# Gate logits as eight more columns of the output product, routing one step earlier

## The reference, cut to what matters

```python
x = x + tanh(g_xattn[0]) * xattn(layernorm(x), ctx, ctx, W_qkv, b_qkv, W_out, b_out)   # 16 heads of 8
x = x + tanh(g_ffn[0])   * moe(layernorm(x), Wg, W1, b1, W2, b2)

# moe: 8 experts, each takes at most 512 of the 4096 tokens, in token order
logits = tokens @ Wg
gates  = softmax(logits);  idx = argmax(gates)
mask1  = one_hot(idx);     loc = cumsum(mask1, axis=0) - 1        # place within the expert
mask1  = mask1 * (loc < 512)
out    = gates1 * (relu(token @ W1[e] + b1[e]) @ W2[e] + b2[e])   # for tokens that got a place
```

## Time and profile before

| | us |
|---|---|
| median of three runs | 356.81 |
| the three runs | 352.88, 356.81, 358.24 |
| the profiled execution | 352.81 |
| its span in the profile | 351.0 |

### The profile page before, as it was taken

One profiled execution on the slowest core, in us unless ns is written; L12 is line 12 of the kernel. 1 busy time (PEld: TensorE's weight loads), 2 busy tenths in 40 slices (PEclk: granted clock), 3 DMA queues, 4 the chain that ended last, 5 costly groups with the idle time before them and its releaser, 6 DMA issues.

```text
span 351.0 us, 8166 instructions
## 1 busy us (share of the span) xinstructions
PE 261.1 (74%) x2960; PEld 169.0 (48%) x2960; DVE 201.8 (57%) x696; ACT 158.5 (45%) x357; POOL 173.4 (49%) x202
## 2 busy tenths in 40 slices
PE   0348698888996995996896888969331899999920
PEld 0124445545654654654654555635220366777720
DVE  6244649778895895568687597932320144544520
ACT  7253376865764763564674456551010332322100
POOL 5336724757179179238728625070462005555572
PEclk9999999999998998589899699995555699999985
DMA  2984765615244235208217111074014225664300
GB/s 79 294 222 110 229 183 149 182 32 162 64 115 129 66 91 152 63 3 230 51 29 209 43 56 64 5 200 76 30 51 130 71 64 162 186 200 142 89 37 21
DMA packets 48536, 39.26 MB, mean 112 GB/s; under 512 B 9619, under 2 KB 44072, under 8 KB 48497
## 3 DMA queue, kind: packets, MB, share of 16 engines
q1 hardware_dynamic: 44784, 28.67, 30.5%
q0 software_dynamic: 3712, 10.07, 8.6%
HBM read 13.72 MB, written 12.65 MB: 75 GB/s over the span
## 4 chain that ended last, share of the span: by engine, by line
POOL 26%; issue 26%; PE 22%; ACT 8%; DVE 7%; DMA 5%; SPq 2%; POOLq 1%; ACTq 0%; DVEq 0%
POOL rec_dram L1002 7%; POOL out_dram L1056 6%; POOL rs L982 4%; PE O L489 3%; PE X L418 3%; ACT prob L623 2%; ACT xn L615 2%; DVE negm L734 2%; POOL rec L988 2%; PE S L460 2%; POOL rec L990 2%; PE X L412 2%; PE TS L561 2%; PE X L435 2%; DMA qp<-parts_q 2%
## 5 line engine op out<-in xcount | busy, mean ns | idle before, releaser
L734 DVE TENSOR_REDUCE negm<-S 128x4 f32<-128x512 f32 x128 | 81.8, 680 | 27.5 <-PE S L460 26.5
L623 ACT ACTIVATE prob<-TS 128x512 f32<-128x512 f32 x128 | 72.0, 589 | 47.5 <-PE TS L475 47.3
L489 PE MATMUL O<-prob,vals 128*32 128x128 f32 x1024 | 58.1, 303 | 1.6 <-ACT oraw L632 1.6
L460 PE MATMUL S<-kp,qp 62*128 62x128 bf16 x512 | 33.5, 234 | 5.2 <-DVE negm L734 4.7
L1056 POOL DMA_INDIRECT out_dram<-fin,tok x32 | 31.3, 979 | 11.2 <-issue 11.2
L1002 POOL DMA_INDIRECT rec_dram<-rec,slot x32 | 31.8, 994 | 9.7 <-issue 9.7
L256 POOL TENSOR_TENSOR rest_k<-full_k,parts_k 128x512 f32<-128x512 f32 x7 | 8.1, 1155 | 53.4 <-ACT parts_k L606 53.4
L489 PEld LDWEIGHTS O<-prob,vals 128*32 128x32 f32 x1024 | 21.3, 113 | 21.7 <-issue 10.9
L975 POOL TENSOR_TENSOR fence_p<-pool_c 128x1 f32<-128x1 f32 x16 | 3.1, 194 | 56.7 <-DVE fin L955 34.3
L460 PEld LDWEIGHTS S<-kp,qp 62*128 62x128 bf16 x512 | 19.2, 100 | 23.5 <-issue 11.7
L475 PE MATMUL TS<-qp,kp 64*128 64x128 bf16 x512 | 28.9, 228 | 1.3 <-DMA qp<-mrow 1.3
(11 more groups left out here) (115 smaller groups left out, 513.1 us busy)
## 6 DMA issues: line engine op xcount, KB each, us to landing
kp<-parts_k SPq DMA_DIRECT2D x48, 128.0 KB
qp<-parts_q SPq DMA_DIRECT2D x48, 128.0 KB, 2.7
rec_dram<-zeros POOLq DMA_DIRECT2D x8, 516.0 KB
xr<-rec_dram SPq DMA_DIRECT2D x8, 260.0 KB, 2.9
c_sb<-in_ctx_dram SPq DMA_DIRECT2D x8, 256.0 KB, 4.4
out_dram<-rec SPq DMA_DIRECT2D x8, 256.0 KB
w1s<-in_L_ffn_W_dram SPq DMA_DIRECT2D x8, 256.0 KB, 3.1
w2s<-in_L_ffn_W_dram SPq DMA_DIRECT2D x8, 256.0 KB, 2.9
```

The lines of the kernel that those rows point to most:

```text
L460: mm = nc.tensor.matmul(S[:, a, i * L:(i + 1) * L], qp[b][rows, h, t0:t0 + L], kp[b][rows, h, t0:t0 + L], start=True, stop=True)
L489: mm = nc.tensor.matmul(o_out[i * HV:(i + 1) * HV, u * L:(u + 1) * L], vals[G % 2][:, k, h, :], prob[n % 2][:, h * L:(h + 1) * L], start=( ...
L623: nc.scalar.activation(prob[n % 2][:, first:first + 4 * L], TS[:, a, :], ACT.Exp).then_inc(a_exp, 1)
L734: V.tensor_reduce(negm[n % 2][:, first:first + 4], S[:, a, :].rearrange("p (h k) -> p h k", k=L), AX.X, ALU.max, negate=True).then_inc(v_r ...
```

## The change

**Logits by linearity.** The output product `onT x wout_g` gets 8 more columns, so that it is [128 x 136]. The added columns of the weights are W_out (times its gain) times the centred gate weights, wg_c = Wg less its mean over the features; they are worked out once, in steps 0 and 1, by two transposes and two small products, and wg_c by a product with a constant matrix in step -6. x's part of the logits comes from the transposed normalised x that the q product uses anyway: a task xl (four matmuls into 8 columns each, step j=0) and one DVE operation (x_logits), which multiplies by the standard deviation sd1. The result stands beside x in x_sb, which has 136 columns now, and so the addition of line 765 yields x1 and the raw logits at once.

**Taken out** in each group: PE's transpose of the second norm (nT, 4 transposes), ACT's copy of it (669), the logits product (lg, 4 matmuls) and DVE's copy (842).

**Added** in each group: xl on PE, x_logits, a second operation in offset1 (sd1) and `scaled` (logit differences times 1/std) on DVE.

**Moved.** route from j=2 to j=0, directly after the group's last residual; pos from j=3 to j=1 (and from 14 small matmuls to 5); place from j=3 to j=2; the exponential from j=2 to j=1; x's statistics and their aggregation from j=0 and j=1 of one group to j=3 of the group before; root(g+2) ahead of norm2(g-2) on POOL; ACT's first half of x's normalisation ahead of the last two exponentials of step j=1. The scatter of group 6 no longer stands behind norm2 of group 7. The bias is added to x one group later.

**The start.** The context of group 0 is loaded second. x is loaded group by group. The statistics of group 0 wait for x alone; the weights are reordered without the gains; the first q split is DVE's instead of POOL's; two of the three q buffers are cleared by POOL instead of ACT; two DVE fills come later; records of zeros are written in steps 1 to 8.

```diff
@@ x_tasks
-            third = {2: ("lg", g - 2), 3: ("pos", g - 2)}.get(j)
+            third = {0: ("xl", g), 1: ("pos", g - 2)}.get(j)
-            second = {1: ("nT", g - 2), 2: ("xT", g + 2), 3: ("q", g + 2)}.get(j)
+            second = {2: ("xT", g + 2), 3: ("q", g + 2)}.get(j)
@@ PE tasks
-                elif name == "nT":
-                    pe.wait_ge(g_xn2, idx + 1)
+                elif name == "xl":
                     for k in range(GB):
-                        mm = nc.tensor.transpose(X[:, 0, k * L:(k + 1) * L], rec[idx % 3][:, k, 0:D], ident)
-                elif name == "lg":
-                    pe.wait_ge(a_nT, idx + 1)
-                        mm = nc.tensor.matmul(X[:, 1, k * E:(k + 1) * E], xn2T[:, k * L:(k + 1) * L], wg_sb[:],
+                        mm = nc.tensor.matmul(X[:, 1, k * E:(k + 1) * E], xnT[idx % 2][:, k * L:(k + 1) * L], wg_c[:],
@@ PE step
-                    nc.tensor.matmul(X[:, 0, 0:D], onT[(c - 5) % 2][:], wout_g[:], start=True, stop=True).then_inc(p_at, 1)
+                    nc.tensor.matmul(X[:, 0, 0:DE], onT[(c - 5) % 2][:], wout_g[:], start=True, stop=True).then_inc(p_at, 1)
@@ DVE
+                V.tensor_tensor(sd1[H % 2][:], rs1[:, 0, :], rs1[:, 1, :], ALU.mult).then_inc(v_sd, 1)
+            def x_logits(H):
+                V.tensor_tensor(x_sb[:, H * GB:(H + 1) * GB, D:DE], X[:, 1, 0:GB * E].rearrange("p (k e) -> p k e", e=E),
+                                sd1[H % 2][:].unsqueeze(2).broadcast_to([P, GB, E]), ALU.mult).then_inc(v_xl, 1)
+            def scaled(G):
+                dve.wait_ge(v_lraw, G + 1)
+                dve.wait_ge(g_rs2, G + 1)
+                V.tensor_tensor(ldif[:], ldif[:], rs2[:, 1, :].unsqueeze(2).broadcast_to([P, GB, E]), ALU.mult).then_inc(v_ldif, 1)
@@ DVE step (order of the group parts)
+                if j == 2 and is_group(g - 2):
+                    positions(g - 2)
                 if is_batch(c):
                     top(c, 0)
 ...
+                if j == 0 and is_group(g):
+                    x_logits(g)
+                if j == 0 and is_group(g - 2):
+                    route(g - 2)
+                if j == 1 and is_group(g - 2):
+                    scaled(g - 2)
                 if j == 2 and is_group(g - 2):
-                    logits(g - 2)
-                if j == 3 and is_group(g - 2):
-                    positions(g - 2)
-                if j == 2 and is_group(g - 2):
-                    route(g - 2)
-                if j == 3 and is_group(g - 2):
                     place(g - 2)
-                if j == 0 and is_group(g + 2):
-                    moments1(g + 2)
+                if j == 3 and is_group(g + 3) and g + 3 >= 2:
+                    moments1(g + 3)
+                    gathered1(g + 3)
@@ POOL step
+                if j == 0 and is_group(g + 2) and g + 2 >= 2:
+                    root(g + 2, mv1, rs1, v_mv1, g_e1).then_inc(g_rs1, 1)
                 if j == 0 and is_group(g - 2):
                     norm2(g - 2)
-                if j == 0 and g - 3 == NG - 2:
-                    scatter(NG - 2)
 ...
-                if j == 3 and is_group(g - 2) and g - 2 != NG - 2:
+                if j == 3 and is_group(g - 2):
                     scatter(g - 2)
@@ SP
-            sp.dma_start(x_sb[:, 0:GB, :], x_v[:, 0:GB, :]).then_inc(x_in[0], 16)
+            sp.dma_start(x_sb[:, 0:GB, 0:D], x_v[:, 0:GB, :]).then_inc(x_in[0], 16)
+            sp.dma_start(c_sb[0][:], ctx_v[:, 0:GB, :]).then_inc(c_in[0], 16)
 ...
-                if c == -7:
-                    sp.dma_start(x_sb[:, 2 * GB:, :], x_v[:, 2 * GB:, :]).then_inc(x_in[2], 16)
+                if j == 1 and 2 <= g + 3 < NG:
+                    rows = slice((g + 3) * GB, (g + 4) * GB)
+                    sp.dma_start(x_sb[:, rows, 0:D], x_v[:, rows, :]).then_inc(x_in[g + 3], 16)
```

More of the change, by code:

```diff
@@ L110, in flamingo_kernel @@
         xn = sb("xn", [P, GB, D])
-        xnT = sb("xnT", [P, GT])
+        xnT = [sb(f"xnT{i}", [P, GT]) for i in range(2)]
         st1 = sb("st1", [P, GB, 6])
@@ L115, in flamingo_kernel @@
         nm1 = sb("nm1", [P, GB])
+        sd1 = [sb(f"sd1_{i}", [P, GB]) for i in range(2)]
         full = [sb(f"full_{s}", [P, GT]) for s in "qk"]
@@ L132, in flamingo_kernel @@
         rs2 = sb("rs2", [P, 2, GB])
[L133 to L135 removed]
+        rec = [sb(f"rec{i}", [P, GB, D + DE]) for i in range(3)]
         lmax = sb("lmax", [P, GB])
@@ L346, in step @@
                     sp.dma_start(out_v[:, sl, :], rec[(g - 2) % 3][:, :, D:2 * D]).then_inc(x1_out[(g - 2) % 3], 16)
-                if loads:
+                if loads and g + 2 >= 1:
                     if g + 2 >= 2:
@@ L498, in step @@
                 at_q = {0: [t for t in groups if t[0] in ("v", "cT") or t[0] == "k" and j == 3], 1: [],
-                        2: [t for t in groups if t[0] in ("lg", "pos", "xT", "q") or t[0] == "k" and j == 2],
-                        3: [t for t in groups if t[0] == "nT"]}
+                        2: [t for t in groups if t[0] in ("xT", "q", "xl") or t[0] == "k" and j == 2],
+                        3: [t for t in groups if t[0] == "pos"]}
                 if is_batch(c):
@@ L652, in step @@
                         first_part(1, 0)
-                if j == 2 and is_group(g + 2):
+                if j == 2 and is_group(g + 2) and g + 2 != 0:
                     normed1(g + 2, (2, 3)).then_inc(a_xn, 1)
+                if c == -5:
+                    act.wait_ge(s_vset, 2)
+                if c == -4:
+                    act.wait_ge(s_gain, 32)
+                    nc.scalar.activation(tg[:], gains[:], ACT.Tanh).then_inc(s_tanh, 1)
+                if j == 1 and is_group(g + 2) and g + 2 >= 2:
+                    normed1(g + 2, (0, 1))
                 if is_batch(c - 2):
@@ L685, in step @@
                     nc.scalar.activation(lexp[:], ldif[:], ACT.Exp).then_inc(a_lexp, 1)
-            for i in range(3):
-                nc.scalar.memzero(qp[i][:]).then_inc(a_pad, 1)
-            act.wait_ge(s_bias, 96)
-            nc.scalar.activation(tg[:], gains[:], ACT.Tanh).then_inc(s_tanh, 1)
-            act.wait_ge(s_vset, 1)
+            nc.scalar.memzero(qp[0][:]).then_inc(a_pad, 1)
             run_steps(step)
@@ L895, in step @@
                     split(dve, V, 1, 0)
-                if j == 0 and is_group(g + 2):
-                    moments1(g + 2)
-                if j == 1 and is_group(g + 2):
-                    offset1(g + 2)
-            for i in range(3):
-                V.memset(kp[i][:].rearrange("p h n -> p (h n)").bitcast(F32), ONES_B).then_inc(v_pad, 1)
-            dve.wait_ge(s_cst, 16)
-            V.tensor_copy(ident_b[:], ident)
-            V.tensor_copy(before_b[:], cst[:, P:2 * P])
-            V.memset(ones_b[:], 1.0)
@@ new lines, in step @@
+                if c == -5:
+                    gathered1(1)
+                    split(dve, V, 0, 0)
+                    offset1(1)
+                if c == -8:
+                    moments1(0)
+                if j == 3 and is_group(g + 3) and g + 3 >= 2:
+                    moments1(g + 3)
+                    gathered1(g + 3)
+                if c == -7:
+                    offset1(0)
+                if c == -7:
+                    dve.wait_ge(s_bias, 64)
+                    V.tensor_scalar(bq_s[:], bqk[:, 0:1], SCALE, None, ALU.mult).then_inc(s_vset, 1)
+                    ones_in(1)
```

220 lines of the change are left out of this document (133 added, 87 removed).

## The result

| | us |
|---|---|
| kernel before, median of five runs | 355.73 |
| changed kernel, median of five runs | 346.10 (345.17 to 348.01) |
| ratio | 0.9753, 95% interval 0.9713 to 0.9792 |
| span of the changed kernel's profiled execution | 346.2 (before 351.0) |

A forecast was written before the change was run, and what follows sets the result against it. PE's waits for POOL's norm2, the lower clock after them and the last group's chain were taken to bound the kernel; terms summing to -32.6 us took 352.81 to 320.2, plus 1 gave 321 us, range 309 to 335.

The forecast's parts named there:

- the 1 us put on the distance of profile and median: Added to the forecast execution of 320.2 us, giving 321; the earlier median lay 4.0 us above the profiled execution.
- to c = 1: Start: earlier loads and statistics, shorter q split on DVE, first score at about 24.6; -6 us (-8 to -3).
- c = 1 to 13, weights folded: Loop before the stalls: added DVE work and xl, +2 us (0 to +4); weight folding, +1 (0 to +2).
- c = 13 to 25: Three stalled groups: 24.5 us each, DVE busy 23.3 setting the pace, against 84.18 in all; -10.7 (-14.3 to -4.7).
- c = 25 to 29: Stretch from 187.29 to 211.96: one stall and lower clock go, 21.0 us instead of 24.67; -3.7 (-5 to -2).
- c = 29 to 32: Stretch from 211.96 to 227.96: shorter stall and routing leave, 14.2 us instead of 16.0; -1.8 (-2.5 to -0.5).
- end of the stage: From 227.96 to 270.88: last scatter starts at 247.5 rather than 260.88; -13.4 us (-16 to -7).
- experts: Expert stage, 80.12 us: not touched by the change.
- rival D: Loop and end: a 3.4 us PE wait per group remains, through the context transpose; 348 to 354 us, chance 0.03.
- collision terms: DVE operations meeting POOL, per stalled group: offset1's two +0.3 us, scaled +0.6, fences of x's statistics +1.0.
- rival B: Loop: POOL's chain (scatter, root, x's offset, normalisation, transpose) keeps groups at 26.6 us; 330 us, chance 0.22.
- the 1.5 us set as the limit: Loop sign: forecast wrong if a DVE wait for POOL's root exceeds 1.5 us per group.

The follow-up runs named there:

- a_ctrl: The changed kernel unaltered, run as a control on chip 5 (quiet): 326.64 us, 0.9375 of before.
- b_pitch: The kernel before with the rows of rec 264 elements apart instead of 258, on a quiet chip: 349.27 us, 0.9964 of before.
- a_fix: The changed kernel with POOL's q split behind nm1 and sd1, and ACT's first normalisations behind the exponentials; quiet chip: 319.80 us, 0.9163 of before.
- a_hold: The changed kernel with POOL's q split of step j=1 waiting for DVE's nm1 and sd1; quiet chip: 320.76 us, 0.9189 of before.
- b_same: The kernel before, unaltered, on chip 8 (held-up): 357.58 us, 1.002 of before.
- a_again: The changed kernel unaltered, run as a control on chip 8 (held-up): 348.78 us, 0.9728 of before.
- a_same: The changed kernel unaltered, run again on chip 2 (held-up): 349.27 us, 0.9753 of before.
- a_layout: The changed kernel with the tiles both kernels have at their old SBUF addresses (rec and x_sb move); quiet chip: 326.13 us, 0.9325 of before.

## Why the prediction was wrong

The direction was right, the size was not: 346.10 us against 321. Three steps of the forecast failed: the price put on c = 1 to 13, the 1 us put on the distance of profile and median, and the sum's premise that with norm2 gone nothing else of PE's stands at the scatter. The terms, on a quiet chip as a_ctrl less b_pitch, and what a held-up chip adds as the changed kernel's first profile less a_ctrl's:

| stretch | forecast | a_ctrl - b_pitch | held-up adds |
|---|---|---|---|
| to c = 1 | -6 | 28.4 - 33.7 = -5.2 | 0.0 |
| c = 1 to 13, weights folded | +2 + 1 | 77.9 - 67.8 = +10.2 | +0.8 |
| c = 13 to 25 | -10.7 | 71.9 - 80.7 = -8.7 | +5.9 |
| c = 25 to 29 | -3.7 | 22.0 - 24.8 = -2.8 | +9.1 |
| c = 29 to 32 | -1.8 | 15.0 - 16.0 = -1.0 | +2.9 |
| end of the stage | -13.4 | 29.3 - 42.8 = -13.5 | +2.7 |
| experts | 0 | 79.7 - 80.3 = -0.6 | +0.5 |
| sum | -32.6 | -21.7 | +21.9 |

The differences are taken before rounding.

- **The start and the end of the stage** were forecast to within 0.8 us on a quiet chip, and by the way they were forecast. The first score starts at 24.53 in a_ctrl, 23.94 in the first profile (24.6 forecast, though its own terms give 24.85; 30.65 in the earlier trace rows). The last four output products take 8.7 us in a_ctrl (8.9), and the fence ahead of the last scatter stands 7.0 us behind the last of them (234.63 less 227.66; 255.91 less 248.93 in the first profile).
- **The stalled groups.** PE's wait for line 990 is gone, so rival D is out. On a quiet chip a group takes 24.0 us, forecast 24.5, but that is luck, not the reason given: DVE is busy 21.61, 21.54 and 20.17 us in them, not 23.3, and the ratio of busy to length is 0.90, 0.90 and 0.84, not 0.95. Two of the three collision terms were too large: nm1 and sd1 took 0.16 and 0.15 us (1.4 together in the forecast), and the fences 0.94 us in the first of these groups, where b_pitch has 0.86 and the forecast added 1.0. The third, scaled, took 0.93 (0.8 in the forecast), and a copy in the place task (line 890), which the forecast did not price, took 0.95 to 1.08 instead of 0.16. POOL's root, as rival B had it, keeps nm1 waiting 0.9 us a group, under the 1.5 us set as the limit. The clock is 0.93 of full, not 1.00. The 84.18 us to which the term was added held one group of 30.99 us, where b_pitch has 26.9: at c = 18 PE ran on at the lower clock in that execution (eight logits products in 1.71 us, 0.96 in b_pitch). Some 3.5 us of the forecast gain (84.18 less 80.66) were this execution's misfortune.
- **The term for c = 1 to 13 was the first step that failed.** The forecast put +2 there for DVE's work and xl, and +1 for the weights. It priced a blocked DVE operation at a half or one POOL operation, and only in the steady groups. The first three groups have no scatter, so POOL reaches the q split (at c = 5 the bias) just when DVE reaches nm1, and at c = 9 nm1 stands for two operations in a row, 2.50 us. The offset had been placed ahead of the maxima that PE waits for. The stretch came out at +10.2 instead of +3. a_fix, with POOL held and ACT's order put back, takes 7.9 of it back and leaves +2.2, near the +3 that was forecast. The zero transfers moved to c = 1 to 8, which the forecast did not price at all, come out only once the block is gone (a_hold at c = 9); their share in the +10.2 isn't shown.
- **The second failure is the median.** The sum was made against the profiled execution, 352.81, and 1 us was added for the 4.0 between it and the median. That difference was a sign: the profile has no remote row, as all those of the quiet chips, while the median of 355.73 is of the other kind (356.14 to 357.98; 348.26 to 350.08 on quiet chips). Which chip the profile came from is not on record, so this is inferred from its rows. The medians of b_same and b_pitch put the distance of the kinds at 8 us.
- **What the median hid decides the size.** On a held-up chip the gain of the three middle groups and of the two stretches behind them, 16.2 us in the forecast and 12.5 on a quiet chip, is used up by late signals: the stretches take 17.8 us more. In the old order these lay for the most part in the wait for norm2, as b_same showed. No rival said that something else stood behind the same wait. The two kinds fit together: the changed kernel gains 21.7 us on a quiet chip and is 21.9 us longer on a held-up one, the kernel before is 8 longer there: -21.7 + 21.9 - 8 = -7.8 us of 357. Measured on such chips were 8.6 and 8.7 us (a_again, a_same).

Of the page "SBUF — State Buffer" of the Trainium skill, section "Who interferes with whom", the sentence on DVE and GpSimd excluding each other is borne out by nm1 (2.50 us beside POOL, 0.15 with POOL held). That it is the later one that waits, as the forecast put it, nm1 doesn't show: its record begins 0.18 us ahead of POOL's first operation, and it ends with the second.

## What to carry to other kernels

A wait that one removes may have covered a second one: ask of a stalled step what else ends in it, and whether it does on every chip. When two unrelated edits give the same large gain, run the unaltered kernel beside them before believing either. A small DVE operation of two SBUF inputs placed where POOL starts a run of tensor operations can cost two of them, 2.5 us, not its own 0.15; let POOL wait for it. And a transfer that is merely moved has to be priced at its new place, by what small transfer it will lie beside.

## What the runs showed of the hardware

- On chips 2 and 8, and in the first measurement, DVE and ACT stood up to 5.6 us (b_same) for PE's signals while POOL ran DMA_INDIRECT; on chips 0, 5 and 11 never. Between the kinds the changed kernel differs by some 22 us of 349, the kernel before by 8 of 357, and a kernel with plain transfers by nothing (317.29 and 317.21).
- The hold shows as "remote" in the waits and in the times of the semaphore updates; the trace puts PE's matmuls at 106.67 and 106.91 as if nothing had happened. In traces with it the list of semaphore updates is also shorter, 4,657 in a_same against 5,660 in a_layout: updates of the DMA queues are missing from it (2,976 against 3,924).
- A POOL indirect DMA of 129 KB took 0.97 to 1.07 us on POOL in a_ctrl and in a_same, on either kind of chip. What differs is when the other engines hear of PE's results meanwhile.
- The 32 packets of 256 bytes of two small transfers took 2.66 us among the packets of a 516 KB transfer (a_hold, 77.81 to 80.47) and 0.37 us ahead of them (a_fix, 80.88 to 81.25).
